# A decoder block's memory recurrence: product and half its sum moved to GpSimd, root and offset kept in another form

## The reference

```python
k = phi(x_norm @ Wk.T)              # 64 features, phi = elu + 1
v = x_norm @ Wv.T                   # 128 features
def step(M, kv):                    # M is 64 x 128, 64 steps, one after the other
    v_pred = einsum('bf,bfd->bd', k_t, M)
    surprise = norm(v_t - v_pred)
    M = M + eta_c * surprise * (k_t outer v_t)
    return ln2(M)                   # minus its mean, by the root of its variance + 1e-5
mem_out = einsum('btf,bfd->btd', phi(x_norm @ Wq.T), M)
output = x + mem_out @ Wout.T
```

## Time and profile before

| | us |
|---|---|
| median of the runs | 1951.23 |
| profiled execution, its own time | 1952.97 |
| its span, first to last instruction | 1951.2 |
| busy in the span: TensorE, VectorE | 1321.5, 1371.5 |
| busy in the span: ScalarE, GpSimd | 1150.6, 977.8 |
| recurrence, about 1250.4 to 1511.4 | 261 |

### The profile page before, as it was taken

The page is one execution under the profiler, slowest core; times in us unless marked ns, Lnnn a source line. Parts: engine busy times, 40 slices in busy tenths (PEclk is TensorE's granted clock), DMA queues, the critical chain, the costliest instruction groups (busy, mean ns, idle before and its releaser), DMA issues. The chain is left out here.

```text
span 1951.2 us, 60363 instructions
## 1 busy us (share of the span) xinstructions
PE 1321.5 (68%) x18142; PEld 1074.2 (55%) x18196; DVE 1371.5 (70%) x4938; ACT 1150.6 (59%) x3372; POOL 977.8 (50%) x1502
## 2 busy tenths in 40 slices
PE   6999995988878838995653999200000787849991
PEld 5677773666656628995652777100000565639991
DVE  5899995777787764453555666499999577755575
ACT  4677773777757626774554555365556465526674
POOL 2777775233327757777862444111111454867663
PEclk9999997999989968997886999655555899979995
DMA  2344442311112213333443445200000422223333
GB/s 74 104 113 110 110 113 71 107 50 49 50 43 71 75 51 91 96 92 108 136 135 97 102 88 103 42 1 1 1 1 1 157 66 66 81 64 87 88 114 116
DMA packets 201501, 152.41 MB, mean 78 GB/s; under 512 B 20482, under 2 KB 188802, under 8 KB 200962
## 3 DMA queue, kind: packets, MB, share of 16 engines
q1 hardware_dynamic: 188034, 123.13, 23.9%
q0 software_dynamic: 13312, 27.49, 4.3%
HBM read 76.54 MB, written 65.54 MB: 73 GB/s over the span
## 5 line engine op out<-in xcount | busy, mean ns | idle before, releaser
L1119 PE MATMUL ffn_run_up_ps<-ffn_run_xt,ffn_run_w_now 128*128 128x128 f32 x1792 | 249.4, 284 | 48.9 <-DVE ffn_run_h L1247 20.4
L1089 POOL DMA_INDIRECT expert_outputs<-ffn_run_y_all,ffn_run_ids x224 | 218.8, 977 | 87.1 <-issue 45.8
L1119 PEld LDWEIGHTS ffn_run_up_ps<-ffn_run_xt,ffn_run_w_now 128*128 128x128 f32 x1792 | 224.5, 197 | 61.6 <-ACT ffn_run_xt L1155 31.6
L838 POOL DMA_INDIRECT tokens_by_expert<-ffn_x_all,ffn_dest x192 | 190.7, 993 | 53.2 <-issue 48.8
L1863 PE MATMUL mixer_m_ps<-mixer_mine,mem_state_coef 128*64 128x64 f32 x4 | 0.5, 334 | 283.3 <-DVE mixer_off_in L2000 283.3
L392 POOL TENSOR_TENSOR cross_k_ex<-cross_kt,k_pack 128x256 f32<-128x256 f32 x128 | 76.7, 621 | 197.8 <-ACT cross_kt L591 197.6
L1128 PE MATMUL ffn_run_y_ps<-ffn_weights,ffn_run_h 128*128 x1216 | 173.1, 276 | 0.7 <-DVE ffn_run_y_all L1264 0.5
L1595 POOL TENSOR_TENSOR recur_rho<-recur_var_eps_new,k_pack 128x1 f32<-128x1 f32 x64 | 34.9, 545 | 247.5 <-DVE recur_var_eps_new L1689 247.5
L1863 PEld LDWEIGHTS mixer_m_ps<-mixer_mine,mem_state_coef 128*64 128x64 f32 x4 | 0.3, 206 | 283.4 <-DVE mixer_ones L1998 283.4
L1128 PEld LDWEIGHTS ffn_run_y_ps<-ffn_weights,ffn_run_h 128*128 128x128 f32 x1216 | 154.5, 193 | 1.1 <-issue 1.1
L1156 ACT COPY ffn_run_w_now<-ffn_weights 128x512 f32 x224 | 139.5, 623 | 0.0
(11 more groups left out here) (337 smaller groups left out, 4685.1 us busy)
## 6 DMA issues: line engine op xcount, KB each, us to landing
ffn_run_x<-tokens_by_expert SPq DMA_DIRECT2D x56, 260.0 KB, 3.0
tokens_by_expert<-fill_zeros SPq DMA_DIRECT2D x32, 292.5 KB, 2.8
ffn_run_yg<-expert_outputs SPq DMA_DIRECT2D x16, 512.0 KB, 4.9
memory_rows<-products_row SPq DMA_DIRECT2D x16, 390.0 KB, 4.6
ffn_weights<-memory_rows SPq DMA_DIRECT2D x16, 390.0 KB
tokens_by_expert<-fill_zeros SPq DMA_DIRECT2D x32, 162.5 KB, 2.6
ffn_weights<-in_pack_ffn SPq DMA_DIRECT2D x1, 4112.0 KB, 14.6
self_turned<-in_x_turned SPq DMA_DIRECT2D x64, 64.0 KB, 1.8
```

Of the source, the lines that this page charges most:

```text
L838: pool.indirect_dma_start(xs[h], bass.IndirectOffsetOnAxis(ap=self.dest[:, r, t:t + 1], axis=0), self.x_all[:, t, :], None)\
L1089: pool.indirect_dma_start(ys, bass.IndirectOffsetOnAxis(ap=ids[:, t:t + 1], axis=0), y_all[:, t, :], None)\
L1119: mm = nc.tensor.matmul(up_ps[t.slot(2)][:, c * P:(c + 1) * P], w_now[:, t.slot(2), c * P:(c + 1) * P], xt[:, t.slot(2), :], start=True, s ...
```

## The change

In `memory_products` the column of sums of each Gram block goes from the last place to the first, so that sums and weights line up (`ket` and `vt` are written from column 1 on).

In `memory_recurrence`:

- `state` holds the offset at place 0 and the weights behind it; one multiplication scales both (`last_scaled`), and the multiply-and-sums take the offset's share with the sum column of `g`.
- The product goes to GpSimd. In step t it multiplies the rows t+2 to 63 by `cv`, padded to an even width, and a second GpSimd instruction adds the two halves of each product row (`parts`, two buffers). VectorE sums what is left in the next step (`common`) and multiplies it by `rho` and the Gram column (`past`).
- What step t's own root adds is a polynomial in that root: `z = square * c_t + past`, `quad = z * c_t + quad_kept`, where `square` is the squared Gram column times the length of v, made on ScalarE one step ahead.
- The scale is `sigma`, a square root on ScalarE, of which VectorE takes the reciprocal. The variance after normalisation follows from `rho` itself: `var_eps = 1 + eps - eps * rho^2`, on ScalarE.

```diff
-                            lhs, rhs = ((kt[:, s2, rows], ket[:, s2, b, :]), (vt[:, s2, b, 0:S], vt[:, s2, b, :]),
-                                        (ket[:, s2, b, 0:S], ket[:, s2, b, :]))[n]
+                            lhs, rhs = ((kt[:, s2, rows], ket[:, s2, b, :]), (vt[:, s2, b, 1:S + 1], vt[:, s2, b, :]),
+                                        (ket[:, s2, b, 1:S + 1], ket[:, s2, b, :]))[n]
...
-                    dve.tensor_scalar(ket[:, t.slot(2), :, 0:S], k_ps[0:F, 0:P].rearrange("p (b s) -> p b s", b=2),
+                    dve.tensor_scalar(ket[:, t.slot(2), :, 1:S + 1], k_ps[0:F, 0:P].rearrange("p (b s) -> p b s", b=2),
...
+        def later(t):
+            return slice(t + 2, S)
 
         @block.gpsimd
         def _(pool):
-            for t in range(S):
-                pool.wait_ge(root_asked, 2 * t + 2)
-                pool.tensor_tensor(v["rho"], v["var_eps_new"], k["half"][:, 0:1], ALU.pow).then_inc(root_ready, 1)
+            for t in range(S - 2):
+                half, rest = t // 2 + 1, S - 2 - t
+                pr = prod[:, 0:rest * 2 * half].rearrange("p (a b) -> p a b", b=2 * half)
+                pool.wait_ge(weights_ready, t + 1)
+                if t:
+                    pool.wait_ge(sums_ready, t)
+                pool.tensor_tensor(pr, g[:, later(t), KK + 1:KK + 1 + 2 * half],
+                                   cv[:, t % 2, 0:2 * half].unsqueeze(1).to_broadcast([P, rest, 2 * half]), ALU.mult).then_inc(multiplied, 1)
+                pool.wait_ge(multiplied, t + 1)
+                if t > 1:
+                    pool.wait_ge(common_ready, t - 1)
+                pool.tensor_tensor(parts[:, (t + 1) % 2, 0:rest * half].rearrange("p (a b) -> p a b", b=half), pr[:, :, 0:half], pr[:, :, half:2 * half],
+                                   ALU.add).then_inc(sums_ready, 1)
...
+            act.activation(v_len[:, :], flat[:, VV + 1:VV + 1 + (S - 1) * (ROW + 1) + 1:ROW + 1], ACT.Sqrt).then_inc(squares, 1)
+            act.wait_ge(squares, 1)
+            act.activation(square[:, 0, 1:S], g[:, 1:S, KK + 1], ACT.Square, scale=v_len[:, 0:1]).then_inc(squares, 1)
+            act.wait_ge(prepared, 1)
...
+                act.wait_ge(root_asked, t + 1)
+                act.activation(state[:, t + 1:t + 2], v["r2c"], ACT.Sqrt, bias=g[:, t, VV + 1 + t:VV + 2 + t]).then_inc(root_ready, 1)
+                if t:
+                    act.wait_ge(kept, 2 * t - 1)
+                    act.activation(v["var_eps"], v["rho2"], ACT.Identity, scale=-LN_EPS, bias=v["one_eps"]).then_inc(kept, 1)
+                    act.wait_ge(kept, 2 * t)
...
+                act.activation(v["sigma"], v["h2"], ACT.Sqrt, scale=state[:, t + 1:t + 2], bias=v["var_eps"]).then_inc(root_ready, 1)
+                if t < S - 2:
+                    act.activation(square[:, (t + 1) % 2, later(t)], g[:, later(t), KK + 2 + t], ACT.Square,
+                                   scale=v_len[:, t + 1:t + 2]).then_inc(squares, 1)
+                if t < S - 1:
+                    act.wait_ge(inverse_ready, t + 1)
+                    act.mul(v["rho2"], v["rho"], v["rho"]).then_inc(kept, 1)
...
+                c_t = state[:, nx:nx + 1]
                 dve.wait_ge(root_ready, 2 * t + 1)
+                need(cross_ready)
+                stt(out=v["h2"], in0=c_t, scalar=dd[:, col], in1=v["cross2"], op0=ALU.mult, op1=ALU.add).then_inc(h2_ready, 1)
+                need(last_scaled)
+                moved = put(stt(out=state[:, 0:1], in0=p_n[:, col], scalar=c_t, in1=state[:, 0:1], op0=ALU.mult, op1=ALU.add))
+                if t == S - 1:
+                    break
+                rest = slice(nx, S)
+                far = slice(nx + 1, S)
+                stt(out=cv[:, t % 2, 0:nx], in0=state[:, 1:nx + 1], scalar=2.0, in1=g[:, nx, VV + 1:VV + 1 + nx],
+                    op0=ALU.mult, op1=ALU.mult).then_inc(weights_ready, 1)
+                need(moved)
+                row_ready = put(tt(row[:, 0:nx + 1], state[:, 0:nx + 1], g[:, nx, KK:KK + nx + 1], ALU.mult))
                 if t:
+                    dve.wait_ge(sums_ready, t)
+                    dve.tensor_reduce(common[:, rest], parts[:, t % 2, 0:(S - nx) * ((t + 1) // 2)].rearrange("p (a b) -> p a b", b=((t + 1) // 2)), AX,
+                                      ALU.add).then_inc(common_ready, 1)
+                need(row_ready)
+                h = put(ttr(out=junk[:, 1, 0:nx + 1], in0=row[:, 0:nx + 1], in1=sv2[:, 0:nx + 1], scale=1.0, scalar=0.0,
+                            op0=ALU.mult, op1=ALU.add, accum_out=v["h"]))
                 if t:
+                    dve.wait_ge(common_ready, t)
+                    past_ready = put(stt(out=past[:, rest], in0=common[:, rest], scalar=v["rho"], in1=g[:, rest, KK + nx],
+                                         op0=ALU.mult, op1=ALU.mult))
                 if t:
+                    need(past_ready)
+                dve.wait_ge(squares, t + 2)
+                z_ready = put(stt(out=z[:, rest], in0=square[:, t % 2, rest], scalar=c_t, in1=past[:, rest], op0=ALU.mult, op1=ALU.add))
+                kv = put(ttr(out=junk[:, 2, 0:nx + 1], in0=row[:, 0:nx + 1], in1=g[:, nx, VV:VV + nx + 1], scale=-2.0, scalar=0.0,
+                             op0=ALU.mult, op1=ALU.add, accum_out=v["kv_neg2"]))
+                need(z_ready)
+                quad_ready = put(stt(out=quad[:, rest], in0=z[:, rest], scalar=c_t, in1=quad_kept[:, rest], op0=ALU.mult, op1=ALU.add))
+                dve.wait_ge(root_ready, 2 * t + 2)
                 if t:
+                    dve.wait_ge(kept, 2 * t)
+                dve.reciprocal(v["rho"], v["sigma"]).then_inc(inverse_ready, 1)
+                need(h, quad_ready)
+                mm = put(stt(out=v["mm"], in0=row[:, 0:1], scalar=v["h"], in1=quad[:, ncol], op0=ALU.mult, op1=ALU.add))
+                dve.wait_ge(inverse_ready, t + 1)
+                if far.start < S:
+                    kept_quad = put(ts(quad_kept[:, far], quad[:, far], v["rho"], v["rho"], ALU.mult, ALU.mult))
                 need(mm, kv)
                 u = put(stt(out=v["u"], in0=v["mm"], scalar=v["rho"], in1=v["kv_neg2"], op0=ALU.mult, op1=ALU.add))
+                last_scaled = put(ts(state[:, 0:nx + 1], state[:, 0:nx + 1], v["rho"], None, ALU.mult))
                 need(u)
                 ts(v["r2c"], v["u"], v["rho"], vv_neg[:, ncol], ALU.mult, ALU.max).then_inc(root_asked, 1)
+                need(last_scaled)
+                cross_ready = put(ttr(out=junk[:, 0, 0:nx + 1], in0=state[:, 0:nx + 1], in1=g[:, nx, PP:PP + nx + 1], scale=2.0 / N_MEM,
+                                      scalar=0.0, op0=ALU.mult, op1=ALU.add, accum_out=v["cross2"]))
             dve.wait_ge(root_ready, 2 * S)
+            need(put(dve.reciprocal(v["rho"], v["sigma"])))
+            need(moved)
+            need(put(ts(coef[:, :], state[:, 1:S + 1], v["rho"], None, ALU.mult)))
+            put(ts(offset, state[:, 0:1], v["rho"], None, ALU.mult))
```

More of the change, by code:

```diff
@@ L1576, in memory_recurrence @@
         g = room[:, 0:S * ROW].rearrange("p (t r) -> p t r", r=ROW)
-        prod = sb("prod", [P, S * S // 4])
-        junk = sb("junk", [P, 3, S])
-        quad = sb("quad", [P, S])
+        flat = g[:, :, :].rearrange("p t r -> p (t r)")
+        prod = sb("prod", [P, S * S // 4 + S])
+        parts = sb("parts", [P, 2, S * S // 8 + S])
+        junk = sb("junk", [P, 3, S + 1])
+        quad, quad_kept, z, past = (sb(n, [P, S]) for n in ("quad", "quad_kept", "z", "past"))
+        square = sb("square", [P, 2, S])
@@ L1580, in memory_recurrence @@
         common = sb("common", [P, S])
-        cv, row, wt, half_gain, gain = (sb(n, [P, S]) for n in ("cv", "row", "wt", "half_gain", "gain"))
-        sv_neg2, p_n, p2_n, dd, vv_neg = (sb(n, [P, S]) for n in ("sv_neg2", "p_n", "p2_n", "dd", "vv_neg"))
-        v = {n: sb(n, [P, 1]) for n in ("off", "off_new", "var", "var_new", "var_eps", "var_eps_new", "r2c", "half", "eps", "pm", "cross2", "u", "h2", "rho", "rho2_even", "rho2_odd",
-                                        "gg", "vm_neg2", "wsv2", "h", "mm", "kv_neg2")}
+        cv = sb("cv", [P, 2, S])
@@ L1585, in memory_recurrence @@
+        state, row, sv2 = (sb(n, [P, S + 1]) for n in ("state", "row", "sv2"))
+        p_n, dd, vv_neg, v_len = (sb(n, [P, S]) for n in ("p_n", "dd", "vv_neg", "v_len"))
+        v = {n: sb(n, [P, 1]) for n in ("var_eps", "r2c", "one_eps", "u", "h2", "sigma", "rho", "rho2", "cross2", "kv_neg2", "h", "mm")}
         v = {n: t[:, :] for n, t in v.items()}
-        step_sem, root_asked, root_ready = sem("steps"), sem("root_asked"), sem("root_ready")
-        cleared, h2_ready, new_terms, scaled_terms = sem("cleared"), sem("h2_ready"), sem("new_terms"), sem("scaled_terms")
@@ L1662, in _ @@
-            need(put(dve.memset(v["var"], 0.0)))
-            dve.memset(junk[:, 0, :], 0.0).then_inc(cleared, 1)
+            put(dve.memset(quad_kept[:, :], 0.0))
+            put(dve.memset(past[:, :], 0.0))
+            put(dve.memset(cv[:, :, :], 0.0))
```

(46 more changed lines are left out.)

81 lines of the change are left out of this document (11 added, 70 removed).

## The result

| | before | after |
|---|---|---|
| median of the runs, us | 1950.92 (4 runs, 1945.7 to 1953.53) | 1984.45 (4 runs, 1982.5 to 1988.47) |
| profiled execution, its own time / span | 1952.97 / 1951.2 | 1982.75 / 1980.9 |
| first to last `h2` (63 steps) | 1253.9 to 1509.7: 255.8 | 1248.0 to 1540.5: 292.5 |
| start of the recurrence to first `h2` | 3.5 | 2.2 |

The ratio is 1.0184, 95% interval 1.0167 to 1.0201: slower, by 33.5 us where 60 were predicted. The time lies in the predicted range, 1958 to 2060, and in the narrower one of the likeliest case, 1975 to 2040; the size is a little over half of what was forecast.

A forecast was written before the change was run, and what follows sets the result against it. VectorE's instruction chain was taken to bound the recurrence. 63 x 2.88 us of chain plus 135 of GpSimd elements made 316.4 against 255.8, +60.6; less 0.9, 2012.7 profiled, 2011 on the median; range 1958 to 2060.

The forecast's parts named there:

- the likeliest case: Recurrence: two-input VectorE and reading GpSimd instructions exclude each other as counted; 1975 to 2040 us, chance 0.66.
- Turn-taking: Recurrence: two-SBUF-input VectorE instructions and GpSimd instructions reading SBUF exclude each other; only GpSimd work under the reduction is free.
- The overlap of the power with L1702: GpSimd's power at 1257.52 beside L1702, which keeps its 0.28; said to show nothing, with one element to read.
- The rival that the engines run side by side: Recurrence: GpSimd reads leave VectorE's two-operand instructions at their lengths; loop 213 us, total time 1907 us, chance 0.14.
- GpSimd's product: Recurrence on GpSimd: 42,656 elements at 2.11 ns; 1,024 elements, 2.16 us plus 0.19 fixed, in a middle step.
- The rival that GpSimd pays by the row: GpSimd's product and sum: some 20 ns more per row adds 78 us, giving 2089 us in total; chance 0.09.
- The half-sum: GpSimd's sum of product halves: 21,328 outputs at 2.11 ns, 1.08 us mid-loop, taking another turn between past and z.
- The rival of the pauses: Recurrence: a third of GpSimd's elements (45 us) falls into VectorE's pauses, giving 1966 us in total; chance 0.07.
- The chain: VectorE's dependent instructions in the recurrence: 2.88 us a step without the reduction, 63 steps.
- The head: Start of the recurrence: gains 0.7 us, ScalarE's table load no longer being behind VectorE's preparation.
- the tail: End of the recurrence: gains about 0.2 us, a reciprocal replacing the power.
- the rival of the table loads: ScalarE in the recurrence: Square evicts the root's table, two loads a step, +20 to +60 us; chance 0.04.

The follow-up runs named there:

- The first experiment: Kernel after, with GpSimd's product and half-sum replaced by memsets of the same outputs with the same waits: 1889.79 us, loop 199.7 us.
- half and half: Kernel after without the half-sum, the product's rows split equally between GpSimd and VectorE, VectorE reducing everything: median 1921.51 us, ratio 0.9856 to the kernel before, loop 228.4.
- all on VectorE: Kernel after with GpSimd's block removed, VectorE making the product and reducing all of it: median 1939.18 us, ratio 0.9946 to the kernel before, loop 248.3.

## Why the prediction was right in kind and too high

*Turn-taking: right.* The prediction had it from two moments: L920 with 0.72 instead of 0.42, and pairs of GpSimd instructions that were lengthened. The first experiment takes GpSimd's reads away and leaves its writes, and both stalls go. What the Trainium skill says in "SBUF — State Buffer", § Who interferes with whom, holds here where it bears on this loop: a VectorE instruction with two SBUF inputs stands beside a GpSimd instruction that reads SBUF and not beside one that only writes it (`h` 184 ns beside memsets, 415 beside copies), and `tensor_reduce` stays out of it (504 ns in both). The overlap of the power with L1702 was rightly not taken as evidence against it. The rival that the engines run side by side is refuted.

*GpSimd's product: right in size, in part by luck.* Expected were near 2.4 us for 1,024 elements and 90.0 us of turns in all. It has 2.20, and its turns cost 63.0 us at `h` and some 26 under the reduction (26.5 by the prediction's own count of that), 89.5 together. Two errors cancel in this. The rate is 1.96 ns an element and not 2.11, (2.20 - 0.19) / 1,024, so the elements of all 62 products are 95.3 less 62 x 0.188 = 83.6 us. But the fixed 0.19 doesn't lie beside the chain as was counted: in the middle step the product begins 0.04 after the reduction and holds `h` until 0.05 after its own end, so that its whole 2.20 counts, of which only `h`'s own length comes off. Rows of two elements cost nothing of their own: the first product, 62 rows of 2, takes 0.41 us, where 188 ns and 124 elements at 1.66 to 2.11 ns give 0.39 to 0.45. The rival that GpSimd pays by the row is refuted.

*The half-sum, counted in full: the term that was mis-sized most, 14 of the 24 us.* The loop was to be 316.4 and is 292.5. The half-sum stood in the sum as 21,328 x 2.11 = 45.0 us, on top of a full chain of 2.88 a step; it stalls `z` by 30.9. In the middle step it is 0.90 (from 1392.09 to 1393.16 for the usual 0.17), where 512 elements were to cost 1.08. The trace of after shows where the rest is. `z` is held nearly to the half-sum's end: it ends at 1393.24, the half-sum at 1393.20, and over all 62 steps the median of that difference is 0.05; it is the same 0.05 between `h` and the product. So when GpSimd is through, `z` doesn't take its own 0.25 once more; about 0.20 of it lies within the hold. The prediction added the hold and the instruction's own length. And the half-sum starts 0.20 before `z` (1391.89 and 1392.09, median of the 62 steps 0.20), while `past` runs and `z` waits for it; that is about the fixed 0.19 which the prediction had rightly left out. Of the half-sum's 55.5 us of busy time, 62 x 0.20 at its start and 62 x 0.20 of `z`'s own length cost nothing: 55.5 - 12.4 - 12.4 = 30.7, against the 30.9 of stall. This is worked out from the timeline; no run varies it.

The rival of the pauses had a third of GpSimd's elements fall where VectorE stands anyway and priced it at 45 us less; the time lies between it and the count as made, but the half-sum's part is explained without pauses other than the 0.20 ahead of `z`.

*The chain: mis-sized by 8 us.* It was 2.88 us a step without the reduction. The first experiment has (199.7 - 26.5) / 63 = 2.75. Two terms carry the difference, `h` and `kv`: such a multiply-and-sum was taken at 0.19 to its follower, from L1697 to L1702, and takes 0.12 (1393.16 to 1393.28 above) and 0.11 (1383.32 to 1383.43 in half and half). Twice 0.07 is the 0.13. The step of before from which the 0.19 was read holds the other value too: behind L1706, which starts at 1376.91, the next instruction starts 0.13 later:

```profile
1377.04 0.19 DVE L1709 TENSOR_TENSOR recur_gain<-recur_half_gain,recur_wt 128x33 f32<-128x33 f32 x1
```

One instance was taken where two of the kind stood side by side. The rest of the 24 us, some 2, is spread over small terms.

*Head, tail, table.* The head gave 1.3 us for 0.7 and the tail 0.2 as said. There is one table load in the whole stretch, the one at 1245.75, though Square and the square root alternate in it; the rival of the table loads is refuted.

*What the prediction didn't ask.* It priced the change as a whole against before. The edits that came along with the move are worth 7.5 us of loop (all on VectorE: 248.3 against 255.8), and of the move itself only the product's part under the reduction was free. Half of the product on GpSimd would have turned the move into a gain of 248.3 - 228.4 = 19.9 us of loop. The half-sum was the poorer half: alone it cost 31.0 us and saved nothing, since the reduction that it shortened was the cover of the product.
